# A two-layer graph kernel: tiles 4 and 5 become a part of their own, tile 6 follows alone

## The reference

```python
h = jnp.maximum(_layernorm(x), 0.0)
x = x + max_over_neighbours(h, adj)          # layer 0: elementwise max of h over the row's neighbours
h = jnp.maximum(_layernorm(x), 0.0)
x = x + gat(h, adj, W, a)                    # layer 1
# gat: h = input @ W;  e[i,j] = leaky_relu(h[i] @ a1 + h[j] @ a2, 0.2), masked by adj
#      elu(softmax(e, axis=1) @ h)
```

## Time and profile before

| what | value |
|---|---|
| median of 3 runs (lowest, highest) | 795.0 us (792.14, 795.56) |
| the profiled execution's own time | 794.1 us |
| its span | 792.1 us |
| mean granted TensorE clock | 0.988 |
| busy TensorE / VectorE / ScalarE / GpSimd | 89% / 91% / 61% / 36% |

### The profile page before, as it was taken

How to read it: one execution, slowest core, us unless ns; L and a number is a source line. 1 busy time by engine, 2 the same in 40 slices (tenths; PEclk the granted TensorE clock), 3 DMA queues, 4 the chain that set the end, 5 groups by cost and what they waited for, 6 DMA issues and landing times.

```text
span 792.1 us, 14762 instructions
## 1 busy us (share of the span) xinstructions
PE 706.9 (89%) x5592; PEld 483.2 (61%) x5592; DVE 723.0 (91%) x1120; ACT 486.0 (61%) x615; POOL 283.7 (36%) x258
## 2 busy tenths in 40 slices
PE   1688999999999999999999999779889999999995
PEld 1344544444444444444444444469789999999995
DVE  8899889999999999999999999999968899998894
ACT  2978888888888888888888888364241221010000
POOL 0612033443443443443443444453320075232030
PEclk9999999999999999999999999899999999999998
DMA  9799777897777777777777763724433434444410
GB/s 305 240 373 364 263 249 221 271 327 222 240 257 215 247 239 228 250 248 215 255 233 227 258 206 91 262 69 149 130 112 120 146 135 170 153 157 160 149 40 16
DMA packets 62856, 162.55 MB, mean 205 GB/s; under 512 B 6400, under 2 KB 11136, under 8 KB 58688
## 3 DMA queue, kind: packets, MB, share of 16 engines
q1 hardware_dynamic: 53776, 138.75, 50.6%
q0 software_dynamic: 9008, 22.82, 11.8%
HBM read 117.51 MB, written 44.04 MB: 204 GB/s over the span
## 4 chain that ended last, share of the span: by engine, by line
PE 46%; ACT 21%; DVE 20%; issue 8%; DMA 2%; POOL 1%; ACTq 0%; DVEq 0%; SPq 0%
PE pick_ps L678 22%; PE pick_ps L578 9%; ACT edge_t L373 9%; DVE acc L836 8%; PE order_ps L559 6%; ACT depth L382 6%; DVE rest L1015 5%; ACT first L381 4%; PE late_ps L591 3%; PE late_ps L550 2%; DVE rest L825 2%; DMA subset_max<-keys 1%; PE late_ps L587 1%; PE late_ps L657 1%; DVE acc L944 1%
## 5 line engine op out<-in xcount | busy, mean ns | idle before, releaser
L836 DVE TENSOR_TENSOR acc<-pick_ps,acc 128x1024 f32<-128x1024 f32 x248 | 302.9, 1222 | 27.6 <-PE pick_ps L578 21.3
L345 POOL DMA_INDIRECT found<-subset_max,entry x192 | 206.3, 1074 | 296.0 <-DVE entry L848 195.7
L1015 DVE SCALAR_TENSOR_TENSOR rest<-depth,curves_sb,stage 128x512 f32<-128x512 f32 x256 | 200.9, 821 | 21.6 <-PE pick_ps L678 5.5
L678 PE MATMUL pick_ps<-keys,rest 128*128 128x129 f32 x1792 | 208.0, 277 | 4.5 <-DVE rest L1015 3.5
L678 PEld LDWEIGHTS pick_ps<-keys,rest 128*128 128x128 f32 x1792 | 204.6, 193 | 9.2 <-DVE rest L1015 6.3
L381 ACT ACTIVATE first<-order_ps,neg 128x1024 f16<-128x1024 f32 x128 | 142.7, 1115 | 60.7 <-PE order_ps L559 57.7
L382 ACT ACTIVATE depth<-order_ps,mid 128x1024 f16<-128x1024 f32 x128 | 141.7, 1107 | 0.0
L373 ACT ACTIVATE edge_t<-late_ps 128x1024 f16<-128x1024 uint16 x128 | 131.1, 1024 | 2.9 <-PE late_ps L550 2.9
L559 PE MATMUL order_ps<-edge_t,order_w 128*128 128x512 f16 x256 | 79.2, 392 | 39.3 <-ACT edge_t L373 31.9
L578 PE MATMUL pick_ps<-first,h_hi 128*128 128x512 f16 x256 | 98.4, 384 | 6.0 <-DVE acc L836 5.9
L550 PEld LDWEIGHTS late_ps<-ident_h,stage 128*128 128x128 f16 x1024 | 69.3, 100 | 49.1 <-DMA stage<-adj 13.3
(11 more groups left out here) (140 smaller groups left out, 575.3 us busy)
## 6 DMA issues: line engine op xcount, KB each, us to landing
stage<-adj SPq DMA_DIRECT2D x64, 1024.0 KB
edge_units<-edge_t SPq DMA_DIRECT2D x64, 512.0 KB
stage<-edge_units SPq DMA_DIRECT2D x32, 1024.0 KB, 4.9
subset_max<-keys POOLq DMA_DIRECT2D x12, 512.0 KB, 8.6
found<-subset_max,entry POOLq DMA_INDIRECT x192
best<-x SPq DMA_DIRECT2D x4, 512.0 KB, 6.3
subset_max<-x POOLq DMA_DIRECT2D x4, 512.0 KB, 8.6
out<-keys POOLq DMA_DIRECT2D x7, 256.0 KB, 3.3
```

What stands on the lines that cost most here:

```text
L345: nc.gpsimd.indirect_dma_start(found[:, n % NG, s, :], None, subset_max, bass.IndirectOffsetOnAxis(entry[:, n, s:s + 1], 0)).then_inc(gath ...
L678: last = nc.tensor.matmul(out_ps(q, b), weight[:, n % WEIGHTS, b * P:(b + 1) * P], wh[:, c, :], start=c == 0 and starts(q, b), stop=c == C ...
L836: V.tensor_tensor(acc[:, q % 2, :], pick_ps[k][:, :], acc[:, q % 2, :], ALU.max).then_inc(raised, 1)
L1015: V.scalar_tensor_tensor(out=weight[:, n % WEIGHTS, :], in0=limit[:, q % 4, :], scalar=slope[:, c:c + 1], in1=units[:, m % EDGES, k * TI:( ...
```

## The change

Tiles 4, 5 and 6 were one part, of 12 blocks; now tiles 4 and 5 are one of 8 blocks and tile 6 one of 4. Moments, root, scales and normalise run once more. `ORDER` keeps its value; only its spelling changes. The side work on TensorE and VectorE gets new places, and the banks of rows and columns of tiles 6 and 7 are swapped, with the waits that guard them.

```diff
-        PARTS = ((0, 1), (1, 2), (2, 4), (4, LAST), (LAST, GR))
+        PARTS = ((0, 1), (1, 2), (2, 4), (4, 6), (6, LAST), (LAST, GR))
-        row_ps = lambda g: banks[(4, 5, 0, 1, 5, 4, 5, 5)[g]]
-        col_ps = lambda g: banks[(6, 6, 4, 5, 4, 5, 4, 4)[g]]
+        row_ps = lambda g: banks[(4, 5, 0, 1, 5, 4, 4, 4)[g]]
+        col_ps = lambda g: banks[(6, 6, 4, 5, 4, 5, 5, 5)[g]]
 # rows(g), its waits
                     elif g == 6:
-                        pe.wait_ge(joined, 5)
+                        pe.wait_ge(col_took, 5)
                     elif g == LAST:
                         pe.wait_ge(folded, TILES)
-                        pe.wait_ge(col_took, 6)
+                        pe.wait_ge(joined, LAST)
 # columns(g), its waits
                     elif g in (4, 5):
-                        pe.wait_ge(joined, g + 2)
+                        pe.wait_ge(joined, 6)
                     else:
-                        pe.wait_ge(col_took, 5 if g == 6 else 7)
+                        pe.wait_ge(col_took, g)
 # sources(q): the waits of q == 3 and q == 4 change places
 # TensorE, in the loop over n, after mix(n)
-                    if n in (18, 20, 27):
-                        rows((18, 20, 27).index(n) + 4)
-                    if n in (40, 42, 46):
-                        columns((40, 42, 46).index(n) + 4)
-                    if n in (42, 46, 50):
-                        project((42, 46, 50).index(n) + 4)
-                    if n == 52:
-                        rows(LAST)
-                    if n == 75:
-                        columns(LAST)
-                    if n == 77:
-                        project(LAST)
+                    if n in (18, 20, 42, 64):
+                        rows((18, 20, 42, 64).index(n) + 4)
+                    if n in (35, 37, 60, 77):
+                        columns((35, 37, 60, 77).index(n) + 4)
+                    if n in (38, 41, 63, 79):
+                        project((38, 41, 63, 79).index(n) + 4)
 # VectorE, in the loop over n, ahead of weigh(n): one line of the table
-                    if n == 31:
+                    if n == 50:
                         merge(6)
                         add(6)
```

More of the change, by code:

```diff
@@ L163, in layers @@
         LAST = GR - 1
-        PARTS = ((0, 1), (1, 2), (2, 4), (4, LAST), (LAST, GR))
+        PARTS = ((0, 1), (1, 2), (2, 4), (4, 6), (6, LAST), (LAST, GR))
         TRIO = 3
-        ORDER = [(q, c) for lo, hi in ((0, 2), (2, 4), (4, 6), (6, LAST), (LAST, GR)) for q in range(TRIO) for c in range(lo * ROWS, hi * ROWS)]
+        ORDER = [(q, c) for lo, hi in ((0, 2),) + PARTS[2:] for q in range(TRIO) for c in range(lo * ROWS, hi * ROWS)]
         ORDER += [(q, c) for q in range(TRIO, TILES) for c in range(C)]
@@ L636, in sources @@
                     elif q == 3:
+                        pe.wait_ge(col_took, GR)
+                    elif q == 4:
                         pe.wait_ge(joined, GR)
-                    elif q == 4:
-                        pe.wait_ge(col_took, GR)
                     elif q > 4:
@@ L1056, in _ @@
                         scales(2)
-                    if n == 11:
+                    if n == 12:
                         search(C - 3)
                         name(C - 3)
-                    if n == 13:
+                    if n == 19:
                         join(C - 6)
[L1062 to L1069, removed]
+                    if n in (22, 25):
+                        merge(n // 3 - 3)
+                        add(n // 3 - 3)
+                    if n in (26, 27):
+                        stat(n - 22)
+                    if n == 28:
+                        moments(3)
+                    if n == 31:
+                        scales(3)
+                    if n == 33:
                         search(C - 2)
                         name(C - 2)
-                    if n in (28, 29):
-                        stat(n - 24)
-                    if n == 31:
+                    if n == 44:
+                        search(C - 1)
+                        name(C - 1)
+                    if n == 46:
+                        join(C - 5)
+                    if n == 48:
+                        fold(TILES - 1)
+                    if n == 50:
                         merge(6)
                         add(6)
-                    if n == 33:
+                    if n == 51:
                         stat(6)
-                        moments(3)
-                    if n == 36:
-                        scales(3)
-                    if n == 40:
-                        search(C - 1)
-                        name(C - 1)
-                    if n == 44:
+                        moments(4)
+                    if n == 54:
+                        scales(4)
+                    if n == 56:
                         join(C - 4)
-                    if n == 48:
+                    if n == 58:
                         join(C - 3)
-                    if n == 52:
+                    if n == 60:
                         dve.wait_ge(entry_ready, C)
@@ L1093, in _ @@
                         V.tensor_scalar(over[:, 1:2], over[:, 0:1], float(WORDS), None, ALU.is_ge).then_inc(over_ready, 1)
-                    if n == 56:
+                    if n == 62:
                         join(C - 2)
-                    if n == 67:
+                    if n == 68:
                         join(C - 1)
@@ L1101, in _ @@
                         stat(LAST)
-                        moments(4)
+                        moments(5)
                     if n == 72:
-                        scales(4)
+                        scales(5)
                     if q == 0 and c % ROWS == 0:
```

## The result

| | before | after |
|---|---|---|
| median, same chip (lowest, highest; runs) | 794.25 us (791.67, 795.98; 10) | 790.81 us (789.77, 791.76; 10) |
| ratio to before, 95% interval | | 0.9957 [0.9944, 0.997] |
| profiled execution, its span | 794.1, 792.1 us | 790.32, 788.3 us |
| mean granted TensorE clock | 0.988 | 0.994 |

The change makes the kernel 3.4 us faster by the medians and 3.8 us by the two spans; 5.2 was forecast. 790.8 lies inside the forecast range of 786.0 to 793.5, 1.8 us above the predicted 789.0. By the ratio the change is worth 0.43% (0.30 to 0.56): clear of zero, and small.

A forecast was written before the change was run, and what follows sets the result against it. Neither TensorE (89%) nor VectorE (91%) alone was the bound; both waited for ScalarE's work on tile 4 before product 48. Profiled 794.1 less 5.2 gave 788.9; forecast 789.0, range 786.0 to 793.5.

The forecast's parts named there:

- The mechanism: Before product 48, ScalarE copies tile 6's columns ahead of tile 4's curves; VectorE waits 4.30 us, TensorE 3.70.
- Product 47: Its start on TensorE: 579.4 instead of 585.17, 5.7 us earlier, with 3.1 us of waits ahead of it.
- Project(5): Tile 5's projection on TensorE: ready at 573.0, its turn at 573.7, so 0.7 us of cover.
- rival D: Tile 5's columns hold tile 4's curves, so the wait before project(5) stays; 790.2 if 2 us later; chance 0.04.
- The table load: ScalarE's load before tile 4's curves: 1.28 us, no drain; with the skill's drain project(5) would wait some 0.7 us.
- Products 48 to 72: TensorE work 24.1 plus waits 2.1 us from product 47; product 72 at 605.7, 5.2 earlier; stretch about even with before.
- Rival A: VectorE is the bound after product 48 and the gain is handed back: 793.9, half of it 791.4; chance 0.22.
- Rival B: Many small TensorE waits bring the clock down in products 48 to 72: slower, 798.8; chance 0.07.
- Product 96: Said to start as much earlier as product 72, which was put 5.2 us earlier.
- the cover of 2.7 us at product 84: Tile 7's scaled copies over at about 616, product 84 due at 618.7; each us beyond would be on the path.
- Rival C: Weights after the merges come sooner, shrinking waits of 3.1 and 2.1 us; without any, 783.7; chance 0.04.
- The step that failed: From product 95 to the kernel's end nothing differs, so the 5.2 us gain carries through to 788.9.

The follow-up runs named there:

- experiment 1: Kernel before with only tile 6 split into its own part, all other side work at its old product: 789.29 us, ratio 0.9933.
- experiment 2: Kernel before, no split, with only the fold, the last four joins and the flag moved as in the change: 794.67 us, ratio 0.9999.
- Experiment 3: Kernel before with 36 unused transposes ahead of tile 5's projection, keeping TensorE busy while it waits: 792.86 us, ratio 0.9981.
- experiment 5: Kernel before with ten extra one-column fills on VectorE at products 120 to 129: 795.81 us, ratio 1.0017.
- experiment 6: Changed kernel with VectorE's wait for the last store moved into the fallback block (early branch): 788.93 us, ratio 0.9926 to before.
- experiment 7: Kernel before with the split and all VectorE and TensorE side work up to product 82 placed anew: 788.20 us, ratio 0.9915.
- experiment 9: Kernel before with only the split, plus VectorE's last-store wait moved into the fallback block: 787.96 us, ratio 0.9916.
- experiment 10: Kernel before with the split, the early branch and a milder spread of side work after product 12: 786.50 us, ratio 0.99.
- experiment 8: The kernel of experiment 7 plus VectorE's last-store wait moved into the fallback block: 789.19 us, ratio 0.9929 to before.

## Why the prediction was right, and what it missed

- **The mechanism** held. ScalarE's move of tile 6 stood ahead of tile 4's curves; with tile 6 in its own part the waits of 4.30 and 3.70 us are gone. Experiments 1 and 2 put the whole gain on the split: alone it saves 6.6 us from product 21 to 96, the change saves 4.8, the fold and the joins moved without it save none.
- **Product 47:** forecast 579.4, measured 579.46. The waits ahead of it were put at 3.1 us; the labelled ones are 1.99 and sit at the same weights, the rest is in gaps too small for a row of their own.
- **Project(5)** was forecast ready at 573.0 with a turn at 573.7; 572.9 and 573.66. The cover of 0.7 us was real, and rival D did not come.
- **The table load.** The row shows 1.28 us from 570.01 and the next activation at 571.31. The drain of the Trainium skill's page (ScalarE: Activation LUTs, What ACT_TABLE_LOAD costs) does not show here.
- **Products 48 to 72:** forecast 26.3 us, measured 26.46. Rival A (VectorE becomes the bound) would have had product 72 at 610.7; it is at 605.92. But part of it was true in a way the prediction did not weigh. It found this stretch "about even" with the old one, which still had the low clock behind the hole in it; without the hole and without the moves the stretch takes 24.1 us (experiment 1), so the moved work costs 2.4 us here and gains 0.7 between products 21 and 47.
- **The clock** stayed at 1.00 from 545 to 660, with waits up to 0.87. Rival B, and with it what the Trainium skill tells of another kernel (TensorE: Matmul & The Clock Gate, "A second HAM failure mode") that frequent micro-idles make it swing, is not borne out in this kernel. Experiment 3 confirms the price of the one drop before: 1.65 read, 1.68 measured at product 72.
- **Product 96:** 5.2 forecast, 4.98 measured. Tile 7's columns, the cover of 2.7 us at product 84: TensorE has no wait there. Rival C found nothing.
- **The step that failed** is "From product 95 on every instruction and releaser is as before." The instructions are the same, but VectorE's program ahead of them is longer, and its branch at the end takes 2.9 us instead of 0.6. It costs 1.2 of the 1.4 us between the 788.9 forecast for the profiled execution and its 790.3; the other 0.2 is product 96. Experiments 5 and 6 show it from both sides.

The forecast of the median, 789.0, missed 790.8 by this 1.2, by 0.2 at product 96, and by the 0.5 by which the runs' median lies above the profiled execution (790.3). Two things in the forecast were not earned. It noted that the profiled execution lay 0.9 below the median of 795.0 and yet took 5.2 off the former; from the median it would have been 789.8. That the ten runs of before have a median of 794.25, next to the profiled 794.1, is luck. And its inner range of 787.3 to 790.8 is said to take the waits of 3.1 and 2.1 us half or one and a half times; that is 2.6 us either way, 786.4 to 791.6. (547.33 + 0.60 is 547.93 and not 547.97; nothing hangs on it.) 791.0 was named as the bound for faster; the median is under it by 0.2, but measured against the runs beside it the gain is 0.43%, under the 0.5% that the bound stood for.

## What to carry to other kernels

A part, batch or group that holds work due at different times makes the early half wait for the late one; split it by due date first, and try that alone before moving anything else, since here the rest of the change took back 1.8 us. Price work moved behind a hole as if the hole were already gone. And look behind the last store: a wait that an engine does only for a path not taken belongs inside that path.

## What the runs showed of the hardware

- A branch over a long block that isn't run is not free. From the branch to the first instruction behind the block TensorE took 3.7 to 4.0 us in all twelve profiles. VectorE took 0.6 us in the three kernels whose last program load stands 42.1 us ahead of the last landing (before, experiments 2 and 3) and 2.9 to 3.0 us in the five where it stands 52.1 to 52.2 ahead and the branch comes after the store (after, twice, experiments 1, 5, 7). In the four with the early branch it took 3.3 to 3.9, beside TensorE's and so all but hidden: in experiments 9 and 10 VectorE still arrived 0.3 and 0.1 us behind TensorE. ScalarE took 0.46 and SyncE 0.53 us in all twelve. That the target lies outside the loaded piece is inferred from these loads; which instruction lies at the edge was not looked for.
- The Trainium skill (Advanced Engine Details and Errata, ISA Cache) tells of a cache of instructions with few, large lines. The loads here, in pieces of 8 KB on VectorE's queue, are of that kind, though not of the 16 KB that it gives for a line. The Trainium skill (Advanced Engine Details and Errata, Control Flow Timing) gives about 108 ns for a compare-and-branch. The branch's own record is shorter on ScalarE, SyncE and VectorE, 45 to 72 ns in every profile, also where VectorE arrives 2.9 us later, while TensorE's own record is 3.6 to 4.0 us long. The time that counts here is not in that figure.
- One hole of 3.7 us brought TensorE's granted clock to its lower level for 3.4 us in two profiles (before, experiment 5) and for 6.8 us in a third with the same hole (experiment 2); what decides between the two stays open.
- The six gathers of a block, issued in a chain, take very different times: with the same table, from the naming of block 31 (580.3 and 580.4) to the last data it took 16.1 us in experiment 7 and 19.1 in 8, and the join 20 products behind the naming went without a wait in the one and stood 2.54 us in the other.
